# A layer of latent attention and routed experts on one core: where the last head's division and the output loads stand among the expert tiles

## The reference

```python
xn  = layernorm(x)
out = x + attention(xn) + experts(xn)

# attention: 16 heads of 32 numbers, causal, keys and values from a latent of 128
c      = layernorm(xh @ Wdkv.T) * ln_g + ln_b
scores = mask((xh @ (Wq @ Wuk.T)) @ c.T / sqrt(128))
oh     = softmax(scores) @ (c @ Wuv) @ Wo_h.T       # per head
attention = concat(oh) @ Wo.T + bo

# experts: 8 of them, each 512 x 512; the two with the largest gate logits count
top_idx = top_k(xn @ gate_w + gate_b, 2)
experts = mean over the two of relu(xn @ expert_w[e] + expert_b[e])
```

## Time and profile before

| | us |
|---|---|
| median of 3 runs | 1656.75 |
| lowest and highest | 1655.73, 1659.14 |
| the profiled execution, its own time | 1657.33 |
| its span in the profile | 1655.6 |
| TensorE busy | 1518.2 (92%) |
| VectorE busy | 1149.1 (69%) |
| ScalarE busy | 902.6 (55%) |
| GpSimd busy | 579.7 (35%) |

### The profile page before, as it was taken

How to read it: one execution, slowest core, us unless ns; L and a number is a source line. 1 busy time by engine, 2 the same in 40 slices (tenths; PEclk the granted TensorE clock), 3 DMA queues, 4 the chain that set the end, 5 groups by cost and what they waited for, 6 DMA issues and landing times.

```text
span 1655.6 us, 44474 instructions
## 1 busy us (share of the span) xinstructions
PE 1518.2 (92%) x12544; PEld 810.8 (49%) x12545; DVE 1149.1 (69%) x2501; ACT 902.6 (55%) x1628; POOL 579.7 (35%) x780
## 2 busy tenths in 40 slices
PE   4788859999999999999999999999999879999787
PEld 2687843444444444444544444444444435555233
DVE  5777878777777777777777777777776234444366
ACT  1566644666666666666666666666666423333000
POOL 1343411444445432232223222222322423332553
PEclk9899987999999999999999999999999989999889
DMA  6488670232223223222322332232232465555687
GB/s 163 150 241 244 204 206 18 60 93 68 68 71 91 68 62 88 78 68 65 94 72 62 83 81 68 66 92 71 65 79 61 124 212 173 171 173 155 217 291 268
DMA packets 161453, 198.02 MB, mean 120 GB/s; under 512 B 45792, under 2 KB 95072, under 8 KB 161024
## 3 DMA queue, kind: packets, MB, share of 16 engines
q1 hardware_dynamic: 124224, 114.99, 23.7%
q10 hardware_dynamic: 24192, 46.72, 10.0%
q0 software_dynamic: 12992, 35.77, 7.4%
HBM read 109.13 MB, written 63.12 MB: 104 GB/s over the span
## 4 chain that ended last, share of the span: by engine, by line
PE 77%; DVE 10%; issue 6%; ACT 3%; DMA 2%; SPq 1%; DVEq 1%; POOL 0%; ACTq 0%; POOLq 0%
PE PS L1270 28%; PE PS L1325 27%; PE PS L1366 11%; PE PS L1390 5%; DVE pm L1077 4%; PE PS L1348 2%; ACT arena L761 1%; DVE arena L959 1%; ACT arena L781 1%; DVE mx L1082 1%; DVE stats L884 1%; PE PS L1251 1%; ACT arena L768 1%; DMA expert_rows<-arena 1%; PE PS L1216 1%
## 5 line engine op out<-in xcount | busy, mean ns | idle before, releaser
L1077 DVE TENSOR_REDUCE pm<-PS 128x1 f32<-128x512 f32 (+3 forms) x1280 | 716.0, 602 | 208.7 <-PE PS L1270 198.7
L842 ACT ACTIVATE arena<-PS 128x512 f32<-128x512 f32 (+1 forms) x1152 | 613.4, 575 | 281.9 <-PE PS L1270 262.3
L1270 PE MATMUL PS<-arena 97*64 97x512 f16 (+7 forms) x5120 | 694.3, 353 | 37.6 <-DVE pm L1077 19.4
L1325 PE MATMUL PS<-arena 128*33 128x512 f32 (+3 forms) x2560 | 634.8, 531 | 1.9 <-POOL arena L622 1.9
L1270 PEld LDWEIGHTS PS<-arena 97*64 97x64 f16 (+1 forms) x5120 | 329.8, 110 | 427.3 <-DVE pm L1077 136.1
L622 POOL TENSOR_SCALAR_AFFINE_SELECT arena<-arena 128x256 f32<-128x256 f32 (+1 forms) x256 | 111.1, 434 | 558.2 <-ACT arena L842 558.2
L1325 PEld LDWEIGHTS PS<-arena 128*33 128x33 f32 x2560 | 159.2, 111 | 81.7 <-POOL arena L622 3.0
L1366 PE MATMUL PS<-w_hi,arena 128*128 x576 | 174.4, 385 | 10.6 <-DVE arena L1128 9.0
L861 ACT ACTIVATE arena<-PS 128x1024 f16<-128x1024 f32 x72 | 73.8, 1025 | 157.1 <-PE PS L1348 154.9
L1270 PE MATMUL PS<-later,deny 128*64 128x128 f16 x1024 | 145.5, 222 | 0.0
L1128 DVE SCALAR_TENSOR_TENSOR arena<-PS,eb_bc 128x512 f32<-128x512 f32 x72 | 49.8, 692 | 128.5 <-PE PS L1366 112.2
(11 more groups left out here) (172 smaller groups left out, 1304.9 us busy)
## 6 DMA issues: line engine op xcount, KB each, us to landing
expert_rows<-arena SPq DMA_DIRECT2D x72, 256.0 KB
comb_hl<-arena SPq DMA_DIRECT2D x256, 64.0 KB
arena<-q_pieces ACTq DMA_DIRECT2D x96, 128.0 KB
arena<-k_pieces ACTq DMA_DIRECT2D x96, 128.0 KB
v_rows<-arena SPq DMA_DIRECT2D x8, 1056.0 KB, 7.1
arena<-v_rows ACTq DMA_DIRECT2D x32, 264.0 KB
arena<-in_x SPq DMA_DIRECT2D x16, 512.0 KB, 5.4
xn_rows<-arena SPq DMA_DIRECT2D x16, 512.0 KB, 4.4
```

Source lines behind the costliest of these rows:

```text
L842: a.activation(probs[kk % 4][:, a_ * CH:a_ * CH + w], PS[:, s2_bank(k, x), 0:w], ACT.Exp, scale=SCALE).then_inc(s["exp_done"], 1)
L1077: v.reduce_max(pm[:, c, r, p:p + 1], PS[:, S1_BANK[n], 0:w], AX).then_inc(s["s1_done"], 1)
L1270: last = t.matmul(PS[h:h + P // 2, bank, cols], lhsT[:, h:h + P // 2], rhs, start=start, stop=stop)
L1325: last = t.matmul(PS[rows_, 6 + c % 2, CH - wds[a]:CH], v_sb[pu % 2][:, j + a, :], probs[pk % 4][:, a * off:a * off + wds[a]], start=p_ in ...
```

## The change

`BESIDE` goes from 2 to 3: VectorE takes six tiles before the last head's division instead of four, and ScalarE eight before the high part instead of six. GpSimd issues the gathers of tiles 8 to 11 before the low part instead of behind it. SP stores tiles 0 to 9 before `keep` instead of 0 to 5, then tiles 10 to 15, and only then waits for `keep` and loads the output weights; the eight residual tiles are loaded one after each of the next eight pairs of stores (tiles 16 to 31) instead of all at once. The loops over the other tiles start later by as many. No transfer and no arithmetic is added or removed.

```diff
--- before.py
+++ after.py
@@ -312,7 +312,7 @@
         NP_ = len(PIECES)
 
 
-        FIRST_ROWS, BESIDE = 16, 2
+        FIRST_ROWS, BESIDE = 16, 3
         PV_LAG, ROW_LAG, BOUNCE_LAG, LOAD_FROM = 2, 1, 2, 1
         S1_FROM = 6
 
@@ -532,14 +532,17 @@
                     sp.wait_ge(s["y_done"], count(i * 2 + u + 1))
                     sp.dma_start(y_dram[ds((i * 2 + u) * P, P), :], y_sb[u]).then_inc(s[f"y_st{u}"], 16)
 
-            for i in range(BESIDE + 1):
+            for i in range(BESIDE + 2):
                 expert_rows(i)
             keep(BH // HPB - 1, HPB - 1)
+            for i in range(BESIDE + 2, BESIDE + 5):
+                expert_rows(i)
             sp.wait_ge(s["o_out"], count(16 * BH))
             sp.dma_start(rest, comb_dram).then_inc(s["comb_in"], 16)
             for q in range(OUT_RING):
+                expert_rows(BESIDE + 5 + q)
                 residual(0, q)
-            with sp.Fori(BESIDE + 1, PT // 2) as i:
+            with sp.Fori(BESIDE + 5 + OUT_RING, PT // 2) as i:
                 expert_rows(i)
             with sp.Fori(0, NT // OUT_RING - 1) as m:
                 for q in range(OUT_RING):
@@ -698,10 +701,11 @@
             for q in range(1, AHEAD_G):
                 gather(0, q)
             add_halves(BH - 1, 1)
-            for q in range(AHEAD_G):
-                gather(1, q)
+            for i in range(1, 3):
+                for q in range(AHEAD_G):
+                    gather(i, q)
             low_part(BH - 1)
-            with pool.Fori(2, PT // AHEAD_G) as i:
+            with pool.Fori(3, PT // AHEAD_G) as i:
                 for q in range(AHEAD_G):
                     gather(i, q)
```

## The result

| | before | after |
|---|---|---|
| median, us | 1657.95 (4 runs) | 1646.08 (4 runs) |
| lowest and highest | 1655.73, 1663.36 | 1645.29, 1647.48 |
| the profiled execution, its span | 1657.33, 1655.6 | 1647.48, 1645.7 |

The ratio of after to before is 0.9925, 95% interval 0.9899 to 0.995: faster by 8 to 17 us. Two later measurements of the same changed kernel gave 0.9915 (0.9900 to 0.9929) and 0.9925 (0.9911 to 0.9938). The forecast, 13.63 us of 1656.75, is a ratio of 0.9918. The measured median, 1646.08, lies 3 us above the forecast of 1643.1: inside the stated range of 1641.0 to 1649.0, but outside the forecast's own 1641.5 to 1645, and next to the 1646.4 of the first rival. The time alone doesn't tell the two apart; the profile does. In median times the three measurements gained 11.9, 15.7 and 12.4 us (1657.95 to 1646.08, 1657.16 to 1641.46, 1656.48 to 1644.11).

A forecast was written before the change was run, and what follows sets the result against it. TensorE was taken to bound the later expert tiles, with stalls before them to recover: 11.56 us from stores ahead of loads plus 2.07 from gathers, 13.63 off 1656.75, gives 1643.1 us; range 1641.0 to 1649.0, the forecast's own 1641.5 to 1645.

The forecast's parts named there:

- the first rival: Keep and weights delay stores, so the stall shrinks but stays: 1646.4 us, or 1648.8 with slow clock; chance 0.14.
- What bounds the kernel: Later expert tiles are TensorE's alone; the change can give back only what the stretch before, 1320 to 1344 us, loses.
- The sum: Expert stage: 11.56 + 2.07 = 13.63 us gained, tile 11 at 1335.78 instead of 1349.41.
- SP's order: Stores ahead of the nine loads end VectorE's wait and the slow clock at tile 10: 11.56 us gained.
- The 1.39 us at tile 8: TensorE's gap from tile 7 to 8, 1.39 us too long, laid to a late gather; the earlier gathers remove it.
- Gathers as a term: Issuing gathers of tiles 8 to 11 before the low part removes the two short stalls: 2.07 us gained.
- The later division at nothing: VectorE's division after tile 5 instead of tile 3 fits: costed at nothing, at most 0.69 us if a gap is missed.
- Keep, weights and residual tiles at nothing: SP's loads now ahead of needed stores: delays taken as zero, residual loads inside the slack even without head start.
- the slack: A store has 6.55 us to land, a lone one takes at most 4.86, so 1.7 us delay costs nothing.
- the slower one: Loads between stores each cost as much as the kept head did: 37.5 us lost for 13.63 won, 1680.6; chance 0.04.
- The end at nothing: The end stage moves forward with the tiles, with the same transfers in it: zero change in length.

The follow-up runs named there:

- the second profiles: Kernel before and changed kernel each run again without edit: stage 229.23 and 215.82 us, ratios to the kernel before 0.9996 and 0.9915.
- e7: Changed kernel with the gathers of tiles 8 to 11 behind the low part again: ratio 0.9966 to the kernel before, stage 224.71 us.
- e6: Changed kernel with output weights and four residual tiles loaded at once behind tile 15's store: ratio 0.9907 to the kernel before, stage 216.80 us.
- e1: Kernel before with SP's new order alone, division, high part and gathers as before: ratio 0.9926 to the kernel before, stage 216.44 us.
- e5: Changed kernel with output weights and all eight residual tiles loaded at once behind tile 15's store: ratio 0.995 to the kernel before, stage 223.34 us.
- e10: Changed kernel with five more residual tiles loaded behind the next five pairs of stores: ratio 0.9919 to the kernel before, end 119.83 us.
- e3: Changed kernel once more, unchanged, for a second profile: ratio 0.9915 to the kernel before, stage 215.82 us, end 119.89 us.

## Why the prediction was right, and where not

**What bounds the kernel: right.** The stretch from 1320 to 1344 us, with tile 10's slow matmuls right behind it, held the whole loss, and the stage now runs at its beat from tile 1 to 71.

**The sum: right.** 13.63 us were predicted for the stage, 229.44 - 215.82 = 13.62 measured, and 13.4 between the second profiles (229.23 and 215.82). The measured medians gained 11.9 to 15.7 us; tile 0's start, its own time and the end scatter by more than the difference. That the first median lies next to the first rival's 1646.4 is such scatter: the gaps which that rival needs are absent.

**Its terms: mis-sized by 1.4 us.** I gave SP's order 11.56 us and the gathers 2.07. Alone they bring 13.0 and 2.5. The 1.39 us at tile 8 belong to both: either edit removes them, and on top of SP's order the rest of the change brings only 0.62. I had put them down to GpSimd's place in the order alone, because GpSimd's row stood before them.

**Gathers as a term: right here, wrong as a price.** With the division later they are not a gain of 2.07 us but a condition. Without them the change loses 8.9 us (e7), since the low part then waits 11.5 us with four gathers behind it.

**The later division at nothing: right.** The ratio with it early is 0.9914. It made the kernel no faster; nothing here shows that it was needed.

**Keep, weights and residual tiles at nothing: right, the slack too small.** I had 0.6 us of the weights' delay against 1.7 free. e6 lost 0.98 where the same figures gave 2.1. The 4.86 us for a lone store were an upper end, and the two runs put the room left by the weights at about 2.5 us. The first rival and the slower one fall with that: e1 and all three profiles of the changed kernel have no gap at tiles 12 to 34. The ring order that the Trainium skill states (DMA: Bandwidth & Descriptors, section on queues, rings and completion order) agrees with e5: 3.1 MB ahead of a store cost TensorE 6.1 us with no wait of SP's for a transfer in between. The lean towards the first rival that I drew from its turns between rings was not borne out, and no run here shows those turns by themselves. The 2.6 us that I worked out from the same page's fit are for the path of transfers that GpSimd issues, and the store is SP's; behind 2.1 and 3.1 MB it took 7.61 and 8.41 us.

**The end at nothing: right within scatter**, 119.9 to 122.9 us against 119.8 to 120.8.

## What to carry to other kernels

A load that nobody needs soon can still set the end, through a store in the same queue whose buffer someone does need; read what stands between the issue of that store and its landing, and put bulk loads behind it in pieces no larger than its slack. Before an instruction that will wait is moved later, look at what is queued behind it: the low part cost little where it stood, and 8.9 us with the gathers left behind it. Where two gaps lie side by side, don't add up what each edit is worth until each has been tried alone.

## What the runs showed of the hardware that I had not expected

- The end, the same instructions in every kernel but e10, took 116.0 to 122.9 us on one chip and 96.6 to 97.7 on the other, while the expert stage agreed within 0.1 us (e6's 216.80 less its one gap of 0.98 is 215.82, as on the first chip). The kernel before had a median of 1635.33 us on the one and 1657.16 on the other. The other chip moved 351 GB/s from 1523 to 1610 us (e6) where the first moved 278 (e3). So ratios are to be compared within a chip, above all for a kernel whose end is made of transfers:

```profile
1523.00:1610.00 87.00, 67.25 (x283) 27.95 (x281) 42.52 (x63) 0.00 (x0) 56.53 (x56) 0.86 0.81 278
```

```profile
1523.00:1610.00 87.00, 80.01 (x371) 36.08 (x369) 60.25 (x91) 0.00 (x0) 65.00 (x64) 0.98 0.96 351
```

- Tile 0 took from 3.04 to 5.95 us with the same 12 matmuls, by the clock it met: 1.00 was granted over it in e5, 0.64 in the first profile after, 0.50 in e10. An idle time of 4.34 us in the middle of the stage was followed by 1.2 GHz (e5, first row 1.03 us), one of 0.82 us was not (e6, 0.60).
- Issuing eight 256 KB loads kept SP busy for 4.72 us, 0.59 each: in e5 the store behind them went out 2.8 us late.
